# A GNN layer with a mixture-of-experts layer behind it: 37 of 425 gathers taken out of the sweep and made from the raw rows while the row table is built

## The reference, cut to what matters

```python
def reference(x, src, dst, edge_type_8, W, bias, gate_w, gate_b, w1, w2, w3):
    # x [3125, 256] f32; 53125 edges sorted by dst; 8 relations; W [8, 256, 256]
    h_all = einsum('ni,roi->rno', layernorm(x), W)
    x = x + segment_sum(h_all[edge_type, src], dst, 3125) + bias
    # 16 experts of width 512, the two best for each node
    ...
```

## Time and profile before

| what | us |
|---|---|
| median of 3 runs (965.34, 966.1, 971.89) | 966.1 |
| the profiled execution, its own time | 968.47 |
| its span in the trace | 966.8 |
| GpSimd busy | 656.3 |
| TensorE busy | 751.2 |
| VectorE busy | 500.5 |
| ScalarE busy | 262.7 |

### The profile page before, as it was taken

How to read it: one execution, slowest core, us unless ns; L and a number is a source line. 1 busy time by engine, 2 the same in 40 slices (tenths; PEclk the granted TensorE clock), 3 DMA queues, 4 the chain that set the end, 5 groups by cost and what they waited for, 6 DMA issues and landing times.

```text
span 966.8 us, 17647 instructions
## 1 busy us (share of the span) xinstructions
PE 751.2 (78%) x4527; PEld 632.3 (65%) x4528; DVE 500.5 (52%) x1328; ACT 262.7 (27%) x390; POOL 656.3 (68%) x614
## 2 busy tenths in 40 slices
PE   0447797877887978878887888287997999999980
PEld 0434686766666766656676767266886888888870
DVE  6975444546454444454444575876442444434448
ACT  4621222223222222232222222421332333323323
POOL 1177777777777777777777770166849878598774
PEclk9975897989888998898898989578998999999995
DMA  8634444445454333343334332255536756474547
GB/s 205 187 104 146 142 143 145 142 142 170 139 151 132 105 104 103 104 132 105 103 105 133 104 103 80 85 185 200 177 123 225 226 184 207 130 245 151 149 145 208
DMA packets 91431, 141.87 MB, mean 147 GB/s; under 512 B 13143, under 2 KB 65835, under 8 KB 91402
## 3 DMA queue, kind: packets, MB, share of 16 engines
q0 software_dynamic: 25680, 70.16, 25.0%
q1 hardware_dynamic: 48800, 56.26, 18.2%
q10 hardware_dynamic: 16922, 15.15, 4.9%
HBM read 108.59 MB, written 32.93 MB: 146 GB/s over the span
## 4 chain that ended last, share of the span: by engine, by line
PE 37%; POOL 28%; issue 16%; DMA 9%; DVE 6%; ACT 1%; POOLq 1%; DVEq 0%; SPq 0%; ACTq 0%
POOL got L541 25%; PE ps L1566 13%; PE ps L1548 7%; PE ps L1415 7%; PE ps L1427 6%; DMA got<-x_tab,gidx 5%; PE ps L1574 2%; DMA acc<-in_x 2%; DMA y_tab<-ffn 1%; POOL part L570 1%; PE ps L1532 1%; DVE ps L1349 1%; DMA x_tab<-got 1%; POOL x_sb L581 1%; POOL part L568 1%
## 5 line engine op out<-in xcount | busy, mean ns | idle before, releaser
L541 POOL DMA_INDIRECT got<-x_tab,gidx x425 | 404.3, 951 | 169.4 <-issue 161.5
L1415 PE MATMUL ps<-hot,got 125*128 125x256 f16 x1700 | 234.6, 300 | 110.4 <-DMA got<-x_tab,gidx 94.8
L1415 PEld LDWEIGHTS ps<-hot,got 125*128 125x128 f16 x1700 | 174.9, 106 | 165.4 <-DMA got<-x_tab,gidx 86.1
L1002 DVE TENSOR_TENSOR store<-store,ps 128x512 f32 x150 | 102.8, 686 | 244.9 <-PE ps L1415 214.3
L1427 PE MATMUL ps<-part,store 128*128 128x256 f32 x800 | 192.4, 402 | 0.5 <-DVE acc L1013 0.5
L1566 PE MATMUL ps<-part,operands 128*128 x696 | 180.6, 410 | 8.5 <-POOL part L570 7.3
L1427 PEld LDWEIGHTS ps<-part,store 128*128 128x128 f32 x800 | 161.2, 205 | 23.0 <-issue 0.6
L1566 PEld LDWEIGHTS ps<-part,operands 128*128 128x128 f32 x696 | 131.2, 195 | 35.0 <-issue 9.3
L984 DVE TENSOR_SCALAR hot<-key_row,pass,drel 125x256 f16<-125x256 f16 x425 | 124.8, 365 | 11.9 <-issue 11.5
L1548 PE MATMUL ps<-part,operands 128*128 x696 | 97.2, 289 | 9.9 <-DVE operands L1288 9.9
L686 ACT ACTIVATE dev<-mv,eps 125x1 f32<-125x1 f32 x25 | 7.4, 294 | 349.5 <-DVE mv L1020 349.5
(11 more groups left out here) (226 smaller groups left out, 558.9 us busy)
## 6 DMA issues: line engine op xcount, KB each, us to landing
store<-in_L_ffn_w SPq DMA_DIRECT2D x48, 512.0 KB, 5.0
y_tab<-ffn SPq DMA_DIRECT2D x9, 896.0 KB, 4.6
y_tab<-ffn ACTq DMA_DIRECT2D x58, 128.0 KB, 2.0
xs_tab<-x_sb SPq DMA_DIRECT2D x14, 512.0 KB, 3.6
ffn<-xs_tab ACTq DMA_DIRECT2D x55, 128.0 KB, 2.2
got<-x_tab,gidx POOLq DMA_INDIRECT x425, 2.8
acc<-in_x SPq DMA_DIRECT2D x5, 560.0 KB
x_tab<-got SPq DMA_DIRECT2D x5, 560.0 KB
```

The lines of the kernel that those rows point to most:

```text
L541: nc.gpsimd.indirect_dma_start(got[:, c, :], None, x_tab, bass.IndirectOffsetOnAxis(ap=gidx[:, col:col + 1], axis=0)).then_inc(gathered[g] ...
L1002: v.tensor_tensor(window, window, ps[:, WIN_BANK[g], :].rearrange("p (q n) -> p q n", n=WIN), ALU.add).then_inc(win_added, 1)
L1415: last = mm(ps[:, WIN_BANK[g], k * KEYS:(k + 1) * KEYS], got[0:CE, c, a * DIM + k * P:a * DIM + (k + 1) * P], hot[0:CE, g % HOT, c - c0, : ...
```

## The change

`HELD = 16` is the last chunk of every turn, and chunk 15 of the odd turns is taken too: 25 + 12 = 37 chunks (`EARLY`). Their source indices are loaded first, turned by PE, and POOL gathers the raw float32 rows of `x` for them into `held` (25) and `odd_held` (12), before it waits for the table. VectorE takes the statistics of these 37 tiles after the edge tables are done and ahead of the sweep. In the sweep ACT normalizes the held tile of the next turn (two activations, four ahead of an odd turn) and DVE writes the low part (one or two subtractions). PE waits for these in place of the gathers of group 5. In the sweep POOL issues 16 gathers in an even turn and 15 in an odd one. SP loads the edge lists one batch later, and the relation weights after the last store to the table; PE makes its `first_spread` matmul ahead of the weight transposes. The loops of ACT and DVE now run two turns in one iteration.

```diff
@@ SP
+            early = src.rearrange("(t c e) -> t c e", c=TC, e=CE)
+            sp.dma_start(early_src[0:TILES, :], early[:, HELD, :]).then_inc(early_in, 16)
+            sp.dma_start(early_src[TILES:EARLY, :], ...chunk HELD - 1 of the odd turns...).then_inc(early_in, 16)
             for n in range(X_LOADS):
-                if n == 2:
+                if n == 3:
...
-            sp.dma_start(w_raw, w_rel.rearrange("r (a p) i -> p (r a) i", p=P)).then_inc(w_in, 16)
             for n in range(X_LOADS):
...
                     sp.dma_start(rows[p0:p1, :, :], got[p0:p1, c0:c0 + LOAD, :]).then_inc(batch_moved[n], 16)
+            sp.dma_start(w_raw, w_rel.rearrange("r (a p) i -> p (r a) i", p=P)).then_inc(w_in, 16)
@@ POOL
-                    for c in range(c0, c1):
+                    for c in range(c0, min(c1, HELD - turn % 2)):
...
+            pool.wait_ge(early_ready, 1)
+            for t in range(EARLY):
+                nc.gpsimd.indirect_dma_start(
+                    held[:, t, :] if t < TILES else odd_held[:, t - TILES, :], None, x,
+                    bass.IndirectOffsetOnAxis(ap=early_idx[:, t:t + 1], axis=0)).then_inc(held_in, 16)
             for n in range(X_LOADS):
                 pool.wait_ge(batch_moved[n], 4 * 16)
@@ ACT
+            def held_rows(v, t, odd=None):
+                act.wait_ge(group_done, v * NG + NG)
+                act.sem_inc(tiles_begun, 1)
+                if odd is not None:
+                    ...
+                    nc.scalar.activation(odd_xn[0:CE, :], rows, ACT.Identity, bias=bias_t, scale=scale_t).then_inc(odd_high, 1)
+                    nc.scalar.activation(got[0:CE, HELD - 1, 0:DIM], rows, ...).then_inc(odd_high, 1)
+                ...
+                nc.scalar.activation(held_xn[0:CE, :], rows, ...).then_inc(held_high, 1)
+                nc.scalar.activation(got[0:CE, HELD, 0:DIM], rows, ...).then_inc(held_high, 1)
...
                     clear_tail(1)
+                    act.wait_ge(held_var, EARLY)
+                    nc.scalar.activation(dev[0:CE, :], mv[0:CE, :, 1], ACT.Sqrt, ...).then_inc(held_dev, 1)
+                    nc.scalar.activation(odd_dev[0:CE, :], odd_mv[0:CE, :, 1], ACT.Sqrt, ...).then_inc(held_dev, 1)
...
-                    with act.Fori(2, TILES - 1) as i:
-                        spread(v0 + i - 1)
-                        move_on(v0 + i, i, (v0 + i + 1) * NG + HALF)
-                        keep_x2(v0 + i - 1, i - 1, b)
-                        clear_old(v0 + i, i)
+                    with act.Fori(1, ODD) as pair:
+                        for at in range(2):
+                            i = pair * 2 + at
+                            held_rows(v0 + i + 1, i + 1, odd=None if at else pair)
+                            spread(v0 + i - 1)
+                            move_on(v0 + i, i, (v0 + i + 1) * NG + HALF)
+                            keep_x2(v0 + i - 1, i - 1, b)
+                            clear_old(v0 + i, i)
@@ DVE
+            dve.wait_ge(held_in, EARLY * 16)
+            for t in range(EARLY):
+                n = t - TILES
+                v.bn_stats((stat[0:CE, t, :] if n < 0 else odd_stat[0:CE, n, :]), ...).then_inc(held_stats, 1)
+            for t in range(EARLY):
+                dve.wait_ge(held_stats, t + 1)
+                v.bn_aggr(...).then_inc(held_var, 1)
+            dve.wait_ge(held_dev, 2)
+            ...two reciprocals, two scalar_tensor_tensor...
+            def held_low(n):
+                dve.wait_ge(held_high, (n + 1) * 2)
+                v.tensor_tensor(got[0:CE, HELD, DIM:], held_xn[0:CE, :], got[0:CE, HELD, 0:DIM], ALU.subtract).then_inc(held_ready, 1)
...
                 for at, (t, g) in enumerate(groups):
+                    if at == HALF + 1 and not last:
+                        if odd is not None:
+                            odd_low((b * GEN_W + w) * ODD + odd)
+                        held_low(v0 + i + 1)
@@ PE
-                pe.wait_ge(gathered[g], (v0 + turn + 1) * (c1 - c0) * 16)
+                if g < NG - 1:
+                    pe.wait_ge(gathered[g], (v0 + turn + 1) * (c1 - c0) * 16)
+                elif odd:
+                    pe.wait_ge(odd_ready, sweep * ODD + pair + 1)
+                    pe.wait_ge(held_ready, v0 + turn + 1)
+                else:
+                    pe.wait_ge(gathered[g], (sweep * (TILES - ODD) + pair + 1) * 16)
+                    pe.wait_ge(held_ready, v0 + turn + 1)
```

More of the change, by code:

```diff
@@ L146, in build @@
         wT = part_flat[:, 0:2 * RO].bitcast(F32).rearrange("p (k n) -> p k n", k=KT)
+        held = part_flat[:, 2 * RO:2 * RO + TILES * DIM].bitcast(F32).rearrange("p (t d) -> p t d", d=DIM)
+        held_xn, odd_xn = (part_flat[:, 2 * RO + (TILES + n) * DIM:2 * RO + (TILES + n + 1) * DIM].bitcast(F32) for n in range(2))
         part12 = part[:, :, 0:W12].rearrange("p s (w k n) -> p s w k n", w=2, k=KT)
@@ L156, in build @@
         first_line = line[:, 2 * CHUNKS:3 * CHUNKS + 1]
+        line_end = 4 * EJ * CE + 3 * CHUNKS + 1
+        early_src, early_f = (room[0:EARLY, line_end + n * CE:line_end + (n + 1) * CE] for n in range(2))
+        early_src = early_src.bitcast(I32)
+        early_idx = sb("early_idx", [P, EARLY], I32)
         ends = sb("ends", [EQ, 2, EJ])
@@ L1090, in add_bias, with turn @@
                                        in1=rows, op0=ALU.mult, op1=ALU.add).then_inc(bias_added, 1)
-            def turn(v0, i, b, w, parts=True, norm=True, last=False, then=None):
+            def turn(v0, i, b, w, parts=True, norm=True, last=False, then=None, odd=None):
                 groups = [(i, g) for g in range(HALF, NG)] + ([] if last else [(i + 1, g) for g in range(HALF)])
@@ L1153, in _ @@
                         add_window(v0, 0, g, w, 0, offs)
-                    turn(v0, 0, b, w, parts=False, norm=False)
+                    turn(v0, 0, b, w, parts=False, norm=False, odd=0)
                     dve.wait_ge(bias_added, (b * GEN_W + w + 1) * X_LOADS)
@@ L1157, in _ @@
                     turn(v0, 1, b, w, norm=False)
-                    with dve.Fori(2, TILES - 2) as i:
-                        turn(v0, i, b, w)
+                    with dve.Fori(1, ODD - 1) as pair:
+                        for at in range(2):
+                            turn(v0, pair * 2 + at, b, w, odd=None if at else pair)
+                    turn(v0, TILES - 3, b, w, odd=ODD - 1)
                     then = in_sweep(b * GEN_W + w)
@@ L1401, in _, with window @@
                 turn_weights(n)
-            pe.wait_ge(first_ready, 1)
-            mm(ps[:, 4, 0:CHUNKS + 1], ones[0:1, :], first_line, start=True, stop=True).then_inc(first_spread, 1)
-            def window(v0, turn, g):
+            def window(v0, turn, g, sweep=0, pair=0, odd=False):
                 c0, c1 = GROUPS[g]
@@ L1466, in _, with turn @@
                 with pe.Fori(0, wins_n) as w:
-                    v0 = (b * GEN_W + w) * TILES
+                    sweep = b * GEN_W + w
+                    v0 = sweep * TILES
                     for g in range(NG):
-                        window(v0, 0, g)
+                        window(v0, 0, g, sweep)
                     for g in range(HALF):
                         window(v0, 1, g)
-                    def turn(i, at, norm=True):
+                    def turn(i, at, pair, norm=True):
                         window(v0, i, 3)
                         window(v0, i, 4)
-                        window(v0, i, 5)
+                        window(v0, i, 5, sweep, pair, odd=at == 1)
                         if norm:
@@ L1493, in _ @@
                     window(v0, t, 4)
-                    window(v0, t, 5)
+                    window(v0, t, 5, sweep, ODD)
                     pe.wait_ge(choice_step, (b * GEN_W + w) * SWEEP_STEPS + 2 * CHOICE_STEPS)
```

75 lines of the change are left out of this document (68 added, 7 removed).

## The result

The changed kernel took 944.31 us (median of 4 runs, 943.81 to 945.85), the kernel before 967.35 on the same chip (4 runs, 965.34 to 971.89). The ratio is 0.975, 95% interval 0.9725 to 0.9776. The forecast was 936, range 926 to 956: the sign and the range held, and the gain is 23 us where 30 were forecast. The profiled execution took 945.85, with a span of 944.1 against 966.8, 22.7 us less. Where the executions of a kernel fell into a faster and a slower group, as on three of the chips further down, its ratio compares the faster ones alone, while its median takes in all.

The account below looks back on a forecast made before the run. GpSimd's gathers were taken to bound the sweep. Its last gather starts 34.5 us earlier; less 4 for the loop, 30.5 off the profiled 968.5 is 938.0. That execution stood 2.4 above the median, hence 936, range 926 to 956.

Parts of the forecast that it names:

- the restart of the gathers: GpSimd fills turn 0, waits 5.0 us for the first window, and goes on with the table's gathers at 77.1.
- later restart: Rival, start: early gathers beside busy VectorE, full DMA queues or late weights; 936 + 8, with both 950; chance 0.18.
- Items 1 to 3: Start on GpSimd, DMA and VectorE: last held row landed at 53.5, statistics follow, first window at 75.3.
- Item 4: Start: late relation weights, turned, copied, then ScalarE's clears, 68 to 76 against 69.5; costed at nothing, else up to 6 us.
- Item 2: DMA engines in the start: 45.1 us of work must fit into 52; the table has until 52.0.
- The cover: Start: VectorE's statistics were to hide the late weights and ScalarE's clears; if that fails, up to 6 us.
- First window to restart: End of the start: the first window, at 75.3, is done after 7.04 / 4 = 1.8 us, at 77.1.
- The loop: Sweep: small losses in odd turns as PE's work must fit shorter turns; 4 us in all, bounds 0 and 22.
- the 0 of that rule: Sweep: if shorter waits keep TensorE's windows at the upper clock level, the 4 us loss would be 0, sum 932.

## Why the prediction was right in sign and 8 us short

**Right.** GpSimd paces the sweep, before and behind the change; 12 gathers more off it gave another 14.4 us. The early gathers fit into the idle start: 6.00 to 53.8 (5.5 to 52.0 forecast). The sweep's 371 steps took 467.8 us (466.0 and 4 lost forecast; 1.8 lost). No wait of PE for held rows appeared among its waits. PE's wait for gathers, 2.8 us a turn, was above the 1 to 2.5 named, since PE's work in a turn came out at 16.3 us (83.33% of a turn of 19.55) and not at 17.0.

**The step that failed is the restart of the gathers, 77.1 forecast and 85.56 measured.** The "later restart" rival named the causes, but the forecast priced them at nothing. Term by term:

- Items 1 to 3, start of the statistics: forecast 53.5, measured 58.83, 5.3 us. Two terms were too small, and each alone accounts for it. The last held row was to land at 50.7 + 2.8; its gather started at 52.58 and took 6.2 us, because the 2.8 is a row of the sweep, where the DMA share is 0.38. And VectorE's own tables were taken as ending at 52.47 as before; they end at 58.81. Item 2 said that the DMA work "fits, barely", and asked only whether the table is late for GpSimd. It was not; but the fourth batch of `x` was late for VectorE. The statistics then took 14.6 and not 15.9, so they end at 73.46, 4.1 later than forecast.
- Item 4, weights at no cost: landed at 62.8, just outside the 54 to 62, and copied by 69.5. ScalarE's clears last up to 76.8, so the roots start 3.2 us after the statistics. This is read from the timeline; no run takes it out alone on a chip of this level. The cover was named, and the sum of the item itself (68 to 76 against 69.5) said that it may fail. The mid of that span should have been taken.
- From the roots to the first window 5.3 us, 5.9 forecast.
- First window to restart: 3.5 us, forecast 1.8. The forecast took a quarter of the 7.04 us of the earlier trace rows, as if its 48 matmuls were of one speed. They are not: the first 14 took 3.17 us in the kernel before and in the change alike (two timelines of PE, before and after, cut off at 60 and at 84.9 us):

```profile
57.18 3.17 PE L1415 MATMUL ps<-hot,got 125*128 125x256 f16 x14 [7.56 <-DVE hot L984]
```

```profile
82.03 3.17 PE L1523 MATMUL ps<-hot,got 125*128 125x256 f16 x14 [13.31 <-DVE hot L1076]
```

At 0.226 us each the window of 12 costs 2.7 us, as in the earlier trace rows, where PE had also stood idle before it; the other 0.8 us up to the restart were at nothing in the forecast.

4.1 + 3.2 - 0.6 + 1.7 = 8.4. The loop gave 2.2 back, the stretch behind the last gather took 1.5, which was not forecast; it is 388.9 to 391.8 in the runs at this level, so it is scatter. 8.4 - 2.2 + 1.5 = 7.7 of the 7.8 us between the forecast 30.5 and the 22.7 of the spans.

**Luck.** The rival "the restart is later" gave 944, and 944.3 was measured, but not by its reckoning: its 8 us were 37 gathers of 1.17 us each beside VectorE, and they cost 1.4 us. Its other causes, late weights and full queues, carry the delay.

**The clock.** PE's share of busy time rose from 79.6 to 83.3 in the earlier trace rows and in its answer above, and its granted clock from 0.88 to 0.94. Behind the 13.31 us without a matmul it was 0.50 from 82 to 86 us, the lower of its two levels, and 1.00 from 88 to 94. The Trainium skill (TensorE: Matmul & The Clock Gate, "Part 1: The HAM clock gate") says that activity releases the throttle. The trace agrees, and the loss of 1.8 us lies between the 0 of that rule and the 4 of the forecast.

**Gathers beside VectorE.** The early gathers, beside a VectorE that was busy for 28.9 of 45 us, took 978 and 1010 ns instead of 951. That is 1.4 us in all, not the 8 of the rival, and it sits in six of them, which took 1.09 to 1.40 us. The timeline shows the longest of these, and a gather from the table that took 1.46:

```profile
40.67 0.76 DVE L965 TENSOR_TENSOR got<-hot,got 125x256 f16<-125x256 f32 x2
40.84 1.40 POOL L578 DMA_INDIRECT odd_held<-in_x,early_idx  x1 [0.30 <-issue]
...
57.48 1.27 DVE L1040 TENSOR_TENSOR key_row<-hot,iota 128x256 f16<-128x256 f32 x1
57.63 1.46 POOL L572 DMA_INDIRECT got<-x_tab,gidx  x1 [0.30 <-issue]
```

The gather beside `key_row` ends 0.34 us after `key_row` does, here as in the earlier trace rows. The Trainium skill (SBUF — State Buffer, "SBUF: two separate sides") says that GpSimd can't write descriptors while VectorE runs an operation that takes the shared port pair. The rows beside these two operations agree with that; which operations of VectorE take the pair, no row here tells. Beside the statistics (L1050) the next gathers took 0.95 us, so for them the rows show no cost.

## What to carry to other kernels

Work that is put into an engine's idle start is paid by the others there: list every load, every table and every first use behind it, and price the order on the engine that must release the first item of the loop (here ScalarE's clears ahead of two short square roots), not only the engine that got the work. Only what the first turns need belongs ahead of the loop; the rest of the statistics showed no cost in turns 0 and 1. A mean of a stretch that begins behind an idle time is no price for its first part. And before any edit at the start of a bound loop is timed, run the unaltered change beside it: where its gain is missing, the loop may have another bound, and such an edit need not show in the time, as in seven runs here.

## What was not expected of the hardware

- Chips stand at two levels, 22 to 27% apart: the same kernel before took 967 to 969 us in the first comparison and on two chips, and 1180, 1219 and 1225 us on three others. GpSimd's gathers are equal on both (951 ns in the kernel before at the one, 951 in the change at the other). What differs is when an engine goes on behind another's result (ScalarE stands up to 9.3 us in the turn shown), and a matmul of the messages takes 454 ns against 390. The cause is open.
- A 2 MB load is not free where the start's DMA share is 0.86: issued ahead of the stores to the table it made the share 0.96, and VectorE's edge tables ended 7.1 us later, while GpSimd's early gathers beside it took at most 1.2 us each.
- The landing of a gather grows from 2.8 to about 5 us beside full queues, 6.2 for the last of them, while GpSimd spends only 3 to 6% more on it.
